# New step orders in two preparation stages of a Perceiver kernel, and the first two experts' weights and rows fetched during routing

## The reference, cut to what matters

```python
logits = jnp.einsum('th,eh->te', x, gate_w)
topk_w, topk_ids = jax.lax.top_k(jax.nn.softmax(logits, axis=-1), K)      # K = 4
topk_w = topk_w / jnp.sum(topk_w, axis=-1, keepdims=True)
buf = jnp.zeros((E, C, D)).at[sorted_eid, pos].set(x[tok], mode='drop')   # C = 256 slots
g, u = jnp.split(jnp.einsum('ech,ehf->ecf', buf, w13), 2, axis=-1)
eo = jnp.einsum('eci,eih->ech', jax.nn.silu(g) * u, w2)
routed = jnp.zeros_like(x).at[tok].add(eo[sorted_eid, pos] * flat_w[order][:, None])
```

## Time and profile before

| what | value |
|---|---|
| median of three runs | 3561.38 us (3558.24 to 3561.42) |
| the profiled execution: its own time | 3526.02 us |
| the profiled execution: its span | 3524.3 us, mean granted TensorE clock 0.944 of full speed |
| busy share of the span | PE 89%, DVE 75%, ACT 64%, POOL 55% |
| DMA | 203.90 MB, mean 58 GB/s |

### The profile page before, as it was taken

How to read it: one execution, slowest core, us unless ns; L and a number is a source line. 1 busy time by engine, 2 the same in 40 slices (tenths; PEclk the granted TensorE clock), 3 DMA queues, 4 the chain that set the end, 5 groups by cost and what they waited for, 6 DMA issues and landing times. The chain is left out here.

```text
span 3524.3 us, 89194 instructions
## 1 busy us (share of the span) xinstructions
PE 3140.6 (89%) x35666; PEld 1965.8 (56%) x35666; DVE 2651.3 (75%) x4062; ACT 2251.4 (64%) x4022; POOL 1930.0 (55%) x2353
## 2 busy tenths in 40 slices
PE   7799999999999869789995799999999999858648
PEld 3356656655665547567763355655665565535425
DVE  6688888888888535648856688888888888738652
ACT  4478878877887644436653478877887887633241
POOL 2277767777776633332215267776776777642200
PEclk9999999999999889789997999999999999869879
DMA  3110000001000020248964200011000101020100
GB/s 116 59 32 22 32 23 31 22 31 33 22 32 22 2 90 2 96 151 304 300 217 112 70 22 32 22 31 32 22 32 22 33 22 32 2 70 1 64 32 24
DMA packets 94029, 203.90 MB, mean 58 GB/s; under 512 B 35429, under 2 KB 44389, under 8 KB 87610
## 3 DMA queue, kind: packets, MB, share of 16 engines
q1 hardware_dynamic: 84922, 173.07, 14.6%
q0 software_dynamic: 8704, 25.19, 2.4%
HBM read 167.77 MB, written 30.46 MB: 56 GB/s over the span
## 5 line engine op out<-in xcount | busy, mean ns | idle before, releaser
L265 POOL TENSOR_TENSOR a_elo<-a_e 128x1024 f16<-128x1024 f32 (+1 forms) x448 | 905.7, 2022 | 173.2 <-ACT a_e L337 172.1
L480 PE MATMUL a_ps_k<-l_wk,a_yh 128*128 128x512 f16 (+1 forms) x1664 | 568.5, 382 | 31.6 <-DVE a_yl L364 27.6
L480 PE MATMUL a_ps_v<-l_wv,a_yh 128*128 128x512 f16 (+1 forms) x1664 | 567.3, 382 | 18.7 <-DVE a_v L392 18.7
L335 ACT ACTIVATE a_e<-a_ps_t 128x1024 f32<-128x1024 f32 (+1 forms) x448 | 430.0, 960 | 131.2 <-PE a_ps_t L548 124.8
L403 DVE TENSOR_REDUCE a_mx<-a_ps_m 128x2 f32<-128x1024 f32 x384 | 467.1, 1216 | 13.0 <-PE a_ps_m L518 12.8
L246 POOL TENSOR_TENSOR a_khat<-a_kc,a_rstd 128x512 f32<-128x512 f32 (+1 forms) x416 | 443.5, 1073 | 16.6 <-PE a_ps_kt L501 6.0
L337 ACT ACTIVATE a_e<-a_ps_t 128x1024 f16<-128x1024 f32 (+1 forms) x448 | 429.1, 958 | 1.6 <-PE a_ps_o L575 1.6
L571 PE MATMUL a_ps_o<-a_v,a_e 128*128 128x65 f16 (+1 forms) x3328 | 359.4, 195 | 18.8 <-POOL a_elo L265 18.8
L364 DVE TENSOR_TENSOR a_yl<-a_y,a_yh 128x256 f16<-128x256 f32 (+1 forms) x416 | 353.3, 850 | 18.5 <-ACT a_yh L293 18.2
L573 PE MATMUL a_ps_o<-a_v,a_e 128*128 128x64 f16 (+1 forms) x3328 | 358.2, 196 | 0.0
L548 PE MATMUL a_ps_t<-a_qb,a_kh 64*128 64x128 f16 x6656 | 341.5, 221 | 18.5 <-ACT a_e L337 13.5
(11 more groups left out here) (404 smaller groups left out, 6555.8 us busy)
## 6 DMA issues: line engine op xcount, KB each, us to landing
f_e_w<-in_m_w SPq DMA_DIRECT2D x32, 1024.0 KB, 7.9
a_y<-in_ctx SPq DMA_DIRECT2D x32, 817.0 KB, 4.8
a_y<-in_ctx SPq DMA_DIRECT2D x32, 768.0 KB, 4.6
f_e_w<-in_m_w SPq DMA_DIRECT2D x32, 512.0 KB, 4.8
eo_dram<-f_e_eo SPq DMA_DIRECT2D x32, 512.0 KB, 4.2
f_raw<-in_f_w SPq DMA_DIRECT2D x2, 2730.0 KB, 12.0
qs_dram<-p_q SPq DMA_DIRECT2D x32, 128.0 KB, 2.3
dca_dram<-p_od SPq DMA_DIRECT2D x16, 256.0 KB, 2.1
```

Source lines behind the costliest of these rows:

```text
L265: pool.tensor_tensor(elo[0:r, t, :, 0:w], e32[0:r, t, :, 0:w], e16[0:r, t, :, 0:w], ALU.subtract)\
L335: act.activation(e32[0:r, t, :, 0:w], ps_t[0:r, :, 0:w], ACT.Exp)
L480: m = pe.matmul(out[0:r, :], part[:, t, c, 0:r], w[:, wpart, c, :], start=(c == 0 and a == 0), stop=(c == KC - 1 and a == 2))
```

## The change

In the preparation, for both layers unless said otherwise: the four `zero` steps go from POOL to ACT, as a copy with scale 0.0, in layer 1 behind `dca_values`, in layer 0 between the first `normal` and `turned` steps. On PE `turn_x(s + 1)` follows `project(s)`, where `turn_x(s + 2)` followed `turn_p(s - 3)`. On ACT a step begins with `turned(s + 1)` and ends with `normal(s + 2)`. On DVE the shift comes behind `q_var` (layer 1) or behind `q_root(0)` and in step 2 (layer 0), and `shares` goes ahead of `q_root`; in layer 1 `arrive(2)` goes ahead of `dca_var`. On POOL in layer 1, `dca_hat` goes ahead of `q_hat(0)` and each gather ahead of the root.

In the routing block SP also loads w13 and w2 of experts 0 and 1, ahead of the store that clears the table; behind its last waits it reads the table back, and POOL, behind its 32 scatters, issues the four gathers of experts 0 and 1. The block ends when their rows have landed. w13 now lies in the memory of `ob`, which nothing else uses until layer 1. The expert block starts without these steps and without waits for them.

```diff
-                def zero(q):
-                    pool.memset(vbd[:, 4 * q:4 * q + 4].rearrange("p b f h d -> p (b f h d)"), 0.0).then_inc(g["zero_ok"], 1)
...
-                    for q in range(4):
-                        zero(q)
                     root(2, 1)
                     gather(4)
-                    q_hat(0)
                     dca_hat(0)
                     dca_hat(1)
-                    root(3, 1)
-                    gather(5)
-                    for u in range(1, TT):
+                    for u in range(TT):
                         q_hat(u)
+                        if u + 5 < TT:
+                            gather(u + 5)
                         if u + 3 < TT:
                             root(u + 3, 1)
-                        if u + 5 < TT:
-                            gather(u + 5)
...
                     dca_keys(1)
+                    arrive(2)
+                    moments(2)
                     dca_var(0)
                     dca_var(1)
-                    arrive(2)
-                    moments(2)
                     dca_root()
...
                 for s in range(TT + 3):
-                    if routed and s + 2 < TT:
-                        shift(s + 2, 1)
-                    if not routed and s == 1:
-                        shift(3, 2)
-                    if not routed and s == 2:
-                        shift(5, 3)
                     if s < TT:
                         q_centred(s)
...
                         q_var(s)
+                    if routed and s + 2 < TT:
+                        shift(s + 2, 1)
...
+                    if 2 <= s < TT + 2:
+                        shares(s - 2)
                     if s < TT:
                         q_root(s)
                     if not routed and s == 0:
+                        shift(3, 2)
                         columns()
...
-                    if 2 <= s < TT + 2:
-                        shares(s - 2)
...
+                    if not routed and s == 2:
+                        shift(5, 3)
...
+                def zero(q):
+                    act.activation(vbd[:, 4 * q:4 * q + 4].rearrange("p b f h d -> p (b f h d)"),
+                                   half[:, 0:1].broadcast_to([P, 4 * 2 * 8 * HD]), ACT.Copy, scale=0.0).then_inc(g["zero_ok"], 1)
+
                 if routed:
                     dca_values(0)
                     dca_values(1)
-                normal(0)
-                turned(0)
-                normal(1)
-                turned(1)
-                if routed:
+                    for q in range(4):
+                        zero(q)
+                    normal(0)
+                    turned(0)
                     dca_square(0)
                     dca_square(1)
+                    normal(1)
                     dca_guess()
+                else:
+                    zero(0)
+                    normal(0)
+                    zero(1)
+                    turned(0)
+                    zero(2)
+                    normal(1)
+                    zero(3)
                 for s in range(TT + 3):
-                    if s + 2 < TT:
-                        normal(s + 2)
+                    if s + 1 < TT:
+                        turned(s + 1)
...
-                    if s + 2 < TT:
-                        turned(s + 2)
...
+                    if s + 2 < TT:
+                        normal(s + 2)
...
                 turn_x(0)
-                turn_x(1)
                 for s in range(TT + 3):
                     if s < TT:
                         project(s)
+                    if s + 1 < TT:
+                        turn_x(s + 1)
...
-                    if s + 2 < TT:
-                        turn_x(s + 2)
...
+                    for e in two:
+                        sp.dma_start(w13[e][:, :, :].rearrange("p k n -> p (k n)"), raw["w13"][e]).then_inc(g["expert_in"], 16)
+                        sp.dma_start(w2[e][:, :], raw["w2"][e]).then_inc(g["expert_in"], 16)
                     sp.wait_ge(g["const"], 1)
                     sp.dma_start(slot_dram.rearrange("(p s) o -> p (s o)", p=P), zero[:, :]).then_inc(g["zero_in"], 16)
...
                     sp.wait_ge(g["scat"], 16 * TT * TOPK)
+                    sp.dma_start(tab[:, :], slot_dram.rearrange("(p s) o -> p (s o)", p=P)).then_inc(g["tab_in"], 16)
+                    sp.wait_ge(g["rows_in"], 64)
...
+                    pool.wait_ge(g["h_out"], 16 * TT)
+                    pool.wait_ge(g["tab_in"], 16)
+                    for e in two:
+                        for j in two:
+                            pool.indirect_dma_start(rows[e][:, j, :], None, h_dram.rearrange("t p d -> (t p) d"),
+                                                    bass.IndirectOffsetOnAxis(ap=tab[:, 2 * e + j:2 * e + j + 1], axis=0),
+                                                    bounds_check=B * S - 1, oob_is_err=False).then_inc(g["rows_in"], 16)
...
-                    sp.dma_start(tab[:, :], slot_dram.rearrange("(p s) o -> p (s o)", p=P)).then_inc(g["tab_in"], 16)
-                    for e in two:
-                        load_13(e)
-                        load_2(e)
...
-                    pool.wait_ge(g["tab_in"], 16)
-                    for e in range(E):
-                        if e >= 2:
-                            pool.wait_ge(g["tr_done"], e - 1)
+                    for e in range(2, E):
+                        pool.wait_ge(g["tr_done"], e - 1)
```

More of the change, by code:

```diff
@@ L1896, in moe_ffn @@
         two = range(2)
+        tab = osb("tab", [P, SLOTS // P], I32)
+        w13 = [env.ob[:, :, :].rearrange("p b n -> p (b n)").rearrange("p (u k n) -> p u k n", u=2, k=2)[:, u] for u in two]
+        w2 = [osb(f"w2{u}", [P, 2 * D]) for u in two]
+        rows = [osb(f"rows{u}", [P, 2, D]) for u in two]
         with ExitStack() as ctx:
@@ L1962, in moe_ffn @@
                      "tr ht_done hth_done htl_done lg_done lgc_done gu_done cnt_done acc_done pos_done posc_done route sidx_done scat "
-                     "next_in silu_done sa_done sah_done sal_done y_done x_done sgu_h sgu_l sd_h sd_l sub_done exp_done").split()
+                     "next_in expert_in tab_in rows_in silu_done sa_done sah_done sal_done y_done x_done sgu_h sgu_l sd_h sd_l sub_done exp_done").split()
             g = {name: sem(name) for name in names}
@@ L1989, in _ @@
                     sp.wait_ge(g["next_in"], 16 * 11)
+                    sp.wait_ge(g["expert_in"], 64)
                     sp.wait_ge(g["h_out"], 16 * TT)
                     sp.wait_ge(g["scat"], 16 * TT * TOPK)
+                    sp.dma_start(tab[:, :], slot_dram.rearrange("(p s) o -> p (s o)", p=P)).then_inc(g["tab_in"], 16)
+                    sp.wait_ge(g["rows_in"], 64)
                 @block.gpsimd
@@ L2275, in moe_ffn @@
             ps_o = ctx.enter_context(nc.psum_tensor(pre + "ps_o", [P, 2, 512], F32))
-            tab = sb("tab", [P, SLOTS // P], I32)
-            w13 = [sb(f"w13{u}", [P, 2, 1024]) for u in two]
-            w2 = [sb(f"w2{u}", [P, 2 * D]) for u in two]
             a13 = [[sb(f"a13{u}{h}", [P, 4, 2 * HID], F16) for h in two] for u in two]
             a2 = [[sb(f"a2{u}{h}", [P, 2, D], F16) for h in two] for u in two]
-            rows = [sb(f"rows{u}", [P, 2, D]) for u in two]
             gt = [[sb(f"gt{u}{h}", [P, 4, 2, P], F16) for h in two] for u in two]
@@ L2286, in moe_ffn @@
             eo = [sb(f"eo{u}", [P, 2, D]) for u in two]
-            names = ("tab_in w13_in0 w13_in1 w2_in0 w2_in1 rows_in0 rows_in1 eo_out0 eo_out1 "
+            names = ("w13_in0 w13_in1 w2_in0 w2_in1 rows_in0 rows_in1 eo_out0 eo_out1 "
                      "w13h_done w13l_done w2h_done w2l_done tr_done gth_done gtl_done gu_done silu_done act_done ah_done "
@@ L2298, in times @@
             def times(e):
-                return 16 * (e // 2 + 1)
+                return 16 * (e // 2)
             with nc.Block() as block:
@@ L2351, in split_13 @@
                     def split_13(e):
-                        act.wait_ge(g[f"w13_in{e % 2}"], times(e))
                         if e >= 2:
+                            act.wait_ge(g[f"w13_in{e % 2}"], times(e))
                             act.wait_ge(g["gu_done"], e - 1)
@@ L2359, in split_2 @@
                     def split_2(e):
-                        act.wait_ge(g[f"w2_in{e % 2}"], times(e))
                         if e >= 2:
+                            act.wait_ge(g[f"w2_in{e % 2}"], times(e))
                             act.wait_ge(g["out_done"], e - 1)
@@ L2390, in evacuate @@
                         if e >= 2:
-                            act.wait_ge(g[f"eo_out{e % 2}"], times(e - 2))
+                            act.wait_ge(g[f"eo_out{e % 2}"], times(e))
                         act.activation(eo[e % 2][:, 0, :], ps_o[:, 0, :], ACT.Copy, scale=1.0 / WSCALE).then_inc(g["eo_a"], 1)
@@ L2479, in evacuate @@
                         if e >= 2:
-                            dve.wait_ge(g[f"eo_out{e % 2}"], times(e - 2))
```

(4 more changed lines are left out.)

2 lines of the change are left out of this document (1 added, 1 removed).

## The result

| kernel | median of its runs | beside it, the kernel before | ratio, 95% interval |
|---|---|---|---|
| changed | 3529.61 us (4 runs, 3527.25 to 3533.36) | 3559.81 us (4 runs, 3551.73 to 3561.42) | 0.9923 [0.9909, 0.9937] |
| changed, second time (e11) | 3527.01 us (4 runs) | 3561.01 us (7 runs) | 0.9909 [0.9891, 0.9927] |

The change is faster by 27 us (22 to 32) in the first comparison and by 32 us (26 to 39) in the second. The forecast was 25 us and 3536.4 us. Compared by their spans alone, the change looks 7 us slower. That contradiction had to be settled.

What follows compares the result with a forecast made beforehand. Hand-overs between engines, not work, were taken to bound routing and layer 1's preparation, and POOL's clears to hold DVE. Gains 5 + 15 + 5 = 25 us off the median 3561.4 gave 3536.4, range 3524 to 3550.

Steps and rivals of the forecast that it cites:

- The base: Whole kernel: runs' median 3561.4 us lies 35 above the profiled execution, little of it in changed stretches; 25 taken off unscaled.
- part 3: Routing to experts: early loads, table read and gathers win 10.9 us, a later block end costs 5.8; gain 5.
- part 2: Layer 1's preparation: earlier first tile and a broken cycle between engines, 9.3 us a tile for 11.45; gain 15.
- Part 1: Layer 0's preparation: clears off POOL and project(0) without turn_x(1) in front bring q_centred(0) to 21.2; gain 5 us.
- The won side: Experts' start: barrier to first product takes 7.5 us in place of 18.4, worth 10.9.
- The lost side: Routing block's end: clearing, scatters, table and gathers end it, so the experts begin 5.8 us later.
- The clearing's queue: SP in routing: 3.1 MB ahead at 414 GB/s delay the clearing 7.6 us; first scatter at 1483.2, not 1478.9.
- (a): Rival, layer 1: q_hat, gather and root in POOL's queue form a new cycle; gain 20 or 14, 3547 us; chance 0.08.
- (b): Rival, routing: the clearing and the gathers' landing eat part 3 wholly; gain 20, 3541 us; chance 0.05.
- (c): Rival, preparations: turn_x(s+1) blocks PE's queue when its tile is late; 15 us slower, 3576; chance 0.04.
- (d): Rival, preparations: prologue leads melt in waits that the present order hides; little left, 3556 us; chance 0.06.

Runs made afterwards that it cites:

- e11: The changed kernel, unchanged, measured a second time: 3527.01 us, ratio 0.9909 to the kernel before.
- e1: The kernel before, unchanged, profiled a second time: 3552.5 us (one run).
- e6: The changed kernel with the four clears back on POOL, new orders and prefetch kept: 3540.90 us (one run).
- e7: The kernel before with only the clears moved from POOL to ACT: 3549.30 us (one run).
- e9: The changed kernel with the clearing store ahead of the expert loads and routing tiles 0 to 3 ahead of 4 to 7: ratio 0.9892 to the kernel before.
- e3: The kernel before with only the prefetch in the routing stage, preparations as before: ratio 0.9990 to the kernel before.
- e2: The kernel before with only the new preparations of both layers, without the prefetch: ratio 0.9936 to the kernel before.
- e5: The changed kernel with the clearing store ahead of the expert loads and only 16 of 32 scatters: 3505.36 us (one run).
- e10: The changed kernel with the clearing store ahead of the expert loads, PE waiting for all scatters before the shared experts: 3530.11 us (one run).

## Why the prediction was right, and where it was not

**The base: a step that failed.** "The median of the runs, 3561.4, lies 35 above; the stretches that change hold little of that." Between the two profiles of the kernel before they hold nearly all of it, 25.9 of the 26.4 us between the spans: 23.2 us in the routing stage and 2.7 in layer 1's preparation (99.4 to 122.6 and 112.7 to 115.4, first profile against e1). A single profile 1% below its own runs was taken for a scaled picture of them. That the 25 us taken off unscaled were near the truth was in part luck: an error of part 3 (2.7 too much) and one of part 2 (2.4 too little) went opposite ways.

**Part 1, forecast 5.** The first tile came where it was placed (21.20), and by e6 and e7 for the two reasons given. Over the nine profiles that have both halves in layer 0 the last addition stands at 93.5 to 96.9, mean 95.7, against 99.8 to 100.1: a gain of 4.2, in the profile of the result 3.2. What was not placed is tile 3. The kbd blocks now stand ahead of turned(3) in ACT's list (timeline of the changed kernel):

```profile
38.71 5.00 ACT L1135 ACTIVATE p_kbd<-p_dsq,head_mask 128x512 f32<-128x512 f32 x8
43.61 0.58 ACT L1069 ACTIVATE p_xt<-p_ps_tr 128x512 f32<-128x512 f32 x1
```

From q_centred(2) at 39.8 to q_centred(3) at 51.2 pass 11.4 us, where the kernel before took 7.7 in its first profile, but 9.8 in e1. That the blocks are its cause is argued from the rows, not tried, and they are not all of it: in e9, whose preparation is the same code, the step took 8.4, and project(3) ran in 3.60 us where it took 4.35 here, with a PEclk of 1.00 from 39 to 52 us in place of 0.87.

**Part 2, forecast 15.** Against the first profile it measured 112.7 - 97.7 = 15.1, with the steps close: q_centred(0) 1.9 gained for 3.3, (1) 3.3 for 4.2, a pitch of 9.64 for 9.3, (7) 15.1 for 15.3. Against the kernel before in its usual executions it is more: 115.4 and 115.2 in e1 and e3, whose pitch was 12.1, against a mean of 97.9: 17.4. The mechanism was right; the term was 2.4 too small because the pitch of the one profile, 11.45, was.

**Part 3, forecast 5.** The two sides were 10.9 won and 5.8 lost. The won side measured 10.5 (18.2 in e1, 7.7). The lost side rested on a step that failed: that clearing, scatters, table and gathers end the stage. They did in the first profile. In all the others of the full kernels the shared experts end last, and PE gets to most of them only when POOL's scatters are through. So a scatter run that ends 5 us later moved the shared experts' end by 6.0 (e11) to 9.2 us (e3 and e6, 108.1), and of the 5 there is 2.3 left (mean routing column of the changed kernel, e11, e3 and e6, 120.3, against 122.6). The clearing's queue itself was read rightly: 4.6 us for the first scatter, forecast 4.3. The same 5 us ran at 410 GB/s in the changed kernel's profile:

```profile
1460.00:1465.00 5.00, 2.98 (x14) 2.72 (x14) 3.78 (x7) 3.68 (x10) 3.08 (x3) 0.50 1.02 410
```

The Trainium skill's page "SBUF — State Buffer", section "A bandwidth-pool intuition that's wrong (but worth ruling out)", gives about 358 GB/s between HBM and a core. The trace disagrees again, with 410.

**The sum.** 4.2 + 17.4 + 2.3 = 23.9 by the rows, 27 (22 to 32) and 32 (26 to 39) by the two sets of runs. The rest is not settled. The stretches that the change does not touch differ by more than that from one execution to the next: "to routing" 1352.5 to 1359.3, "rest" 1553.8 to 1564.3. For the former the clock is seen to differ. From 1205 to 1305 us the granted share was 0.73 in e1 and 0.64 in e11, and PE was busy 4.5 us more for fewer matmuls (columns as rows 1):

```profile
1205.00:1305.00 100.00, 57.80 (x932) 45.87 (x926) 30.41 (x43) 46.05 (x63) 42.10 (x30) 0.73 0.24 80
```
```profile
1205.00:1305.00 100.00, 62.33 (x866) 49.93 (x863) 27.55 (x36) 44.77 (x60) 42.19 (x30) 0.64 0.25 80
```

The same DVE reciprocal of the attention starts at 1209.5 in e1 and at 1204.7 in e11: layer 0's lead is there. The routing stage starts at 1452.4 and 1454.4: in this pair it is gone.

**The rivals.** (a) fell: the pitch was 9.64, and DVE's wait for roots 5.0 us. (Its "14 with the bounds of the other parts" does not add up either: 2 + 9.6 + 0 is 12, as the range has it.) (b), part 3 eaten, came nearest: half of it was, though not by the landing of the gathers but by the shared experts behind the scatters. (c) fell: PE waits 1.6 us for normalized tiles in layer 1. (d) fell with e2.

## What to carry to other kernels

Before costing an edit on one profile, put its own time beside the runs: if it lies outside them, find the stage that holds the difference (or take a second profile): here that stage had another bound in the usual execution. Where two changes free one step (the engine that was held, and the queue in front of it), neither shows a gain alone, so try them together before dropping one. And a small store on which a long serial run of DMA issues depends goes ahead of the megabytes in its queue: the 32 KB clearing behind 3.1 MB cost the stage 6 to 9 us of the 10.5 that the prefetch won, though the runs do not settle how much of that the whole kernel gets back.

## What was not expected of the hardware

While POOL issued its 32 indirect scatters (one each 1.28 us), PE, on dense float16 matmuls of 128 columns, came to a crawl after 39 to 41 of them and resumed 3.7 (e9) to 4.8 us (e3) after the last scatter began; gaps of "issue" in front of PE sum to 17.1 us in e1, and no matmul itself took longer than 0.31 us from 1500 to 1525 us. Waits of the changed kernel and of e1 in that stretch (waiter, what for: total, times, longest):

```profile
PE f_ps_gu L2244 <- issue: 22.1, 20, 2.5
```
```profile
PE f_ps_gu L2227 <- issue: 17.1, 18, 1.9
```

The DMA engines moved next to nothing then (1 GB/s in e1, 2 in the changed kernel's profile, 3 in the first). e5 and e10, one profile each, tie the crawl to the long run of scatters, not to every scatter; how the one slows the other is open, and so is why one profile of twelve, the first, ran through them with no gap at all. The gathers in pairs in the experts' stage show nothing of the kind. No edit tried here keeps PE going beside the 32 scatters.
